# One-hot matrices stored by one edge pass and loaded by the next, and joined seams, in a four-layer graph stack on one core

## The reference

```python
h = jnp.maximum(_layernorm(x), 0.0);  x = x + L0(h, src, dst, ...)             # 3 attention layers, 4 heads
h = jnp.maximum(_layernorm(x), 0.0);  x = x + L1(h, src, dst, node_vec, ...)   # attention + scan, gated merge
h = jnp.maximum(_layernorm(x), 0.0);  x = x + L2(h, src, dst, edge_weight, ...)
h = jnp.maximum(_layernorm(x), 0.0);  x = x + L3(h, ...)
```

```python
s     = leaky_relu(a1[dst] + a2[src])
alpha = exp(s - max) / segment_sum(exp(s - max), dst)
agg   = segment_sum(alpha * ft[src], dst)
```

## Time and profile before

| | us |
|---|---|
| median of three runs | 8077.06 |
| the profiled execution, its own time | 8047.32 |
| its span | 8045.5 |
| busy: PE / DVE / POOL / ACT | 5416 / 5247 / 4576 / 3255 |
| L0's pass, gathers to last sum | 922 to 2640 |
| L1's pass with the scan | 3352 to 4960 |
| merge | 4961 to 5545 |
| L2's and L3's passes | 5558 to the end |

### The profile page before, as it was taken

One profiled execution on the slowest core, in us unless ns is written; L12 is line 12 of the kernel. 1 busy time (PEld: TensorE's weight loads), 2 busy tenths in 40 slices (PEclk: granted clock), 3 DMA queues, 4 the chain that ended last, 5 costly groups with the idle time before them and its releaser, 6 DMA issues. The chain is left out here.

```text
span 8045.5 us, 108971 instructions
## 1 busy us (share of the span) xinstructions
PE 5416.1 (67%) x20075; PEld 3414.8 (42%) x20075; DVE 5247.3 (65%) x11331; ACT 3255.3 (40%) x10996; POOL 4576.3 (57%) x4404
## 2 busy tenths in 40 slices
PE   4656788888888346477777774775566665566664
PEld 4523344444444232244444442564344443344443
DVE  7678588888888545698898984563455553333332
ACT  1224566666666225478787873441000000000000
POOL 4140266566665350287777774223777775777774
PEclk9988899999999658798998987897788887788887
DMA  7123577777777553477677776122444445344445
GB/s 256 23 71 107 184 241 243 239 241 243 245 243 219 183 176 96 157 235 243 239 249 241 248 227 147 62 69 72 118 142 142 140 142 96 112 136 136 136 135 88
DMA packets 481482, 1352.15 MB, mean 168 GB/s; under 512 B 129207, under 2 KB 220603, under 8 KB 480506
## 3 DMA queue, kind: packets, MB, share of 16 engines
q0 software_dynamic: 239680, 842.82, 36.1%
q1 hardware_dynamic: 198828, 436.55, 16.0%
q10 hardware_dynamic: 42668, 69.51, 2.8%
HBM read 1133.35 MB, written 546.45 MB: 209 GB/s over the span
## 5 line engine op out<-in xcount | busy, mean ns | idle before, releaser
L1190 POOL DMA_INDIRECT rows_e<-bundle,unit_src x1856 | 1775.2, 956 | 647.2 <-issue 542.2
L1211 PE MATMUL acc_e<-rows_e,hot_e 128*128 128x256 f32 x3712 | 1210.4, 475 | 920.7 <-DMA rows_e<-bundle,unit_src 746.1
L608 POOL DMA_INDIRECT rows_e<-table,unit_src x928 | 1027.6, 1107 | 840.8 <-PE acc_e L797 459.3
L797 PE MATMUL acc_e<-rows_e,hot_e 128*128 128x512 f32 (+1 forms) x3712 | 1343.0, 512 | 174.8 <-DVE rows_e L779 98.2
L967 POOL DMA_INDIRECT rows_e<-table,unit_src x928 | 1157.8, 1248 | 450.1 <-issue 247.1
L1211 PEld LDWEIGHTS acc_e<-rows_e,hot_e 128*128 128x128 f32 x3712 | 816.6, 234 | 1283.3 <-issue 618.7
L786 ACT ACTIVATE rows_e<-rows_e 128x64 f32<-128x64 f32 x4640 | 1119.0, 333 | 1.9
L797 PEld LDWEIGHTS acc_e<-rows_e,hot_e 128*128 128x128 f32 x3712 | 698.1, 195 | 746.3 <-issue 602.0
L1220 DVE SCALAR_TENSOR_TENSOR sums_e<-sums_e,unit_keep,acc_e 128x256 f32<-128x256 f32 x928 | 442.2, 477 | 736.0 <-PE acc_e L1211 730.8
L1053 ACT ACTIVATE rows_e<-rows_e 128x64 f32<-128x64 f32 x3712 | 919.9, 333 | 3.8
L2357 ACT ACTIVATE turned_f<-turn_f 128x512 f32<-128x512 f32 x98 | 58.5, 597 | 1893.2 <-PE turn_f L2355 1836.1
(11 more groups left out here) (444 smaller groups left out, 8525.6 us busy)
## 6 DMA issues: line engine op xcount, KB each, us to landing
bc<-bc_rows SPq DMA_DIRECT2D x226, 896.0 KB
summed<-sums_e SPq DMA_DIRECT2D x464, 390.0 KB
bundle<-sums_e SPq DMA_DIRECT2D x928, 128.0 KB
summed<-sums_e SPq DMA_DIRECT2D x464, 130.5 KB
given_f<-bundle ACTq DMA_DIRECT2D x98, 384.0 KB
rows_e<-table,unit_src POOLq DMA_INDIRECT x1856, 5.0
rows_e<-bundle,unit_src POOLq DMA_INDIRECT x1856, 2.7
summed<-zeros POOLq DMA_DIRECT2D x50, 390.0 KB, 17.6
```

The source lines that it names most:

```text
L608: pool.indirect_dma_start(self.rows[:, v, e, :], None, table, bass.IndirectOffsetOnAxis(unit_src[:, u, e:e + 1], 0)).then_inc(self.landed[ ...
L797: mm = pe.matmul(self.acc[:, v % 2, a0:a1], self.hot[:, v % self.SUMS, e, :], self.rows[:, v, e, a0:a1], start=(e == 0), stop=(e == 1))
L1190: pool.indirect_dma_start(self.rows[:, v, e, :], None, self.tab, bass.IndirectOffsetOnAxis(unit_src[:, u, e:e + 1], 0)).then_inc(self.land ...
L1211: mm = pe.matmul(self.acc[:, v % 2, 0:D], self.hot[:, v % self.SUMS, e, :], self.rows[:, v, e, :], start=(e == 0), stop=(e == 1))
```

## The change

- L0's `one_hot` makes the matrices in a ring of 8 units instead of 4, of which one half lies in the memory of `unit_w`. `unit_w` is therefore stored to DRAM before L0's pass (`w_kept`) and loaded again after it.
- SP stores every pair of units' matrices to DRAM (`hots`, 256 KB a store, 232 stores). DVE waits for the store before it writes over a pair.
- L1's pass has no `one_hot`; SP loads the matrices of four units at a time (512 KB, 116 loads) into a ring of 16 units, and PE waits for the load.
- In L1 `spread_top` stands ahead of `sum_rows` on PE, and `negate_top` at the end of DVE's slot.
- At the half's end, the copy of `y_ps` moves into the first step of the next half (after ACT's `decay`), the clearing matmuls behind that step's edge work on PE, and the gate loads behind the second step's `bc` load. Halves with c = 0 are written out too.
- Merge: the `settle` behind the weight loads goes; one gather of `y_all` is issued with each turn of the lanes; DVE, ACT and PE wait for the weights only where the first block needs `gat_b`. The DVE step on `unit_src` is done here.
- L2: only PE and DVE wait for the six weights. L2's and L3's passes use L0's semaphores for the landed rows again.

```diff
@@ SegmentPass (L0)
-                self.hot = lsb(f"hot_{name}", [P, self.SUMS, 2, P])
+                self.hot = (lsb(f"hot_{name}", [P, self.HOTS // 2, 2, P]),
+                            unit_w[:, :, :].rearrange("p (k u) e -> p k (u e)", k=self.HOTS // 2).rearrange(
+                                "p k (e n) -> p k e n", e=2))
...
+            def store_hots(self, i, v):
+                if v % 2 == 0:
+                    return
+                u, at_, half = i * RING + v, v % self.HOTS, self.HOTS // 2
+                sp.wait_ge(self.s_hot, u + 1)
+                sp.dma_start(hots[:, ds(u - 1, 2), :].rearrange("p u n -> p (u n)"), ...
+                             ).then_inc(self.hot_out[at_ // 2], 16)
...
             def one_hot(self, i, v):
                 u = i * RING + v
-                dve.wait_ge(self.s_pe, u + RING - self.SUMS + 1)
+                dve.wait_ge(self.s_pe, u + RING - self.HOTS + 1)
+                stored = RING // self.HOTS * i + v // self.HOTS
+                if v % 2 == 0 and (not isinstance(stored, int) or stored):
+                    dve.wait_ge(self.hot_out[v // 2 % (self.HOTS // 2)], 16 * stored)
...
                 self.behind(self.store_sums, self.STORE, i, v, edge)
+                self.behind(self.store_hots, self.WEIGH + 1, i, v, edge)
@@ ScoredPass (L1)
-            def one_hot(self, i, v): ...
+            def load_hots(self, i, v):
+                sp.dma_start(self.hot[:, v:v + self.LOAD, :, :].rearrange("p u e n -> p (u e n)"),
+                             hots[:, ds(i * RING + v, self.LOAD), :].rearrange("p u n -> p (u n)")
+                             ).then_inc(self.hot_in[v // self.LOAD % 2], 16)
...
-                pe.wait_ge(self.s_hot, u + 1)
+                k = v // self.LOAD
+                pe.wait_ge(self.hot_in[k % 2], 16 * (RING // self.LOAD // 2 * i + k // 2 + 1))
...
                 self.behind(self.store_sums, self.STORE, i, v, edge)
+                if v % self.LOAD == 0 and edge != "last":
+                    self.load_hots(i, v)
...
+                if j == 2 and edge != "last":
+                    self.spread_top(i, g)
                 self.behind(self.sum_rows, self.SUM, i, v, edge)
-                if edge != "last":
-                    if j == 1:
-                        self.turn_highest(i, g)
-                    elif j == 2:
-                        self.spread_top(i, g)
+                if j == 1 and edge != "last":
+                    self.turn_highest(i, g)
@@ scan
+            def copy_sum(half):
+                act.wait_ge(s_whole, half + 1)
+                act.wait_ge(s_gated, 2 * half + 2)
+                act.activation(y_sb..., y_ps[:, :, 0:HS], ACT.Copy).then_inc(s_copied, 1)
+
+            def clear_sum(half):
+                pe.wait_ge(s_copied, half + 1)
+                for z in range(2):
+                    pe.matmul(y_ps[:, z, 0:HS], zeros[:, 0:P], zeros[:, 0:HS], start=True, ...)
...
                     load_bc(STEPS * r + k + 2, k % 2)
+                    if w == 0 and k == 1:
+                        load_gate(half, g, c)
...
                     make_decay(r, k, m, 2 * f + c)
+                    if w == 0 and k == 0:
+                        copy_sum(half)
...
                     edges.pe_slot(i, v + 1)
+                    if w == 0 and k == 0:
+                        clear_sum(half)
                     add_up(r, k)
@@ merge
-        settle()
...
-            for t in range(T):
-                pool.indirect_dma_start(y_all[:, t, :], None, sorted_y, ...)
+            def return_rows():
+                for t in range(T):
+                    yield pool.indirect_dma_start(y_all[:, t, :], None, sorted_y, ...)
...
-            for e in (sp, pool, pe, dve, act):
-                chain.wait(e)
-                e.wait_ge(merge_loaded, 16 * (len(names) + len(sides) + 5))
+            chain.wait(act)
...
+                if b0 == 0:
+                    for e in (dve, act, pe):
+                        e.wait_ge(weights_here, all_loaded)
...
-            in_lanes(lanes, merge, 8)
+            in_lanes(lanes, merge, 8, return_rows(), 1)
@@ L2
-            chain.dma(sp, l1, l2, l3, l4, l5, l6)
+            for load in (l1, l2, l3, l4, l5, l6):
+                load().then_inc(weights_here, 16)
+            for e in (pe, dve):
+                e.wait_ge(weights_here, all_loaded + 16 * 6)
```

More of the change, by code:

```diff
@@ L215, in graph_stack_kernel @@
         key_row = scratch("key_row", [NP])
+        w_kept = scratch("w_kept", [P, UC * 2])
+        hots = scratch("hots", [P, UNITS, 2 * P])
         by_time = {n: scratch(f"scan_{n}", [P, 2, NP]) for n in ("xc", "dt", "dtx")}
@@ L907, in run @@
                 sp.wait_ge(self.masked[0], 16 * (n + 1))
+                for k in range(self.HOTS // 2):
+                    sp.wait_ge(self.hot_out[k], 16 * (UNITS // self.HOTS))
                 nc.all_engine_barrier()
@@ L940, in __init__ @@
                 self.landed = [sem(f"landed_{name}{v}") for v in range(G)]
+                self.hot_in = [sem(f"hot_in_{name}{k}") for k in range(2)]
                 self.stored = [sem(f"stored_{name}{v}") for v in range(self.SUMS)]
                 (self.s_score, self.s_row, self.s_run, self.s_top, self.s_neg, self.s_shrink, self.s_exp, self.s_keep,
-                 self.s_mark, self.s_hot, self.s_act, self.s_pe, self.s_sum) = (sem(f"{n}_{name}") for n in (
-                     "score", "row", "run", "top", "neg", "shrink", "exp", "keep", "mark", "hot", "act", "pe", "sum"))
+                 self.s_mark, self.s_act, self.s_pe, self.s_sum) = (sem(f"{n}_{name}") for n in (
+                     "score", "row", "run", "top", "neg", "shrink", "exp", "keep", "mark", "act", "pe", "sum"))
                 pe.sem_inc(self.s_pe, RING)
@@ L1114, in dve_slot @@
                 self.behind(self.collect, self.COLLECT, i, v, edge)
+                if j == 3 and edge != "last":
+                    self.negate_top(i, g)
             def act_slot(self, i, v, edge=None):
@@ L1172, in __init__ @@
                 self.acc = lps(f"acc_{name}", [P, 2, 512])
-                self.landed = [sem(f"landed_{name}{v}") for v in range(RING // 2)]
+                self.landed, self.seen = landed, seen
                 self.stored = [sem(f"stored_{name}{v}") for v in range(self.SUMS)]
@@ L2158, in scan_half @@
                 half = 2 * g + c
-                load_gate(half, g, c)
-                pe.wait_ge(s_copied, half + 1)
-                for z in range(2):
-                    pe.matmul(y_ps[:, z, 0:HS], zeros[:, 0:P], zeros[:, 0:HS], start=True, stop=False, skip_group_check=True)
-                if c == 0:
-                    with nc.Fori(0, MR // 2, engines=NOT_POOL) as w:
-                        scan_round(g, f, turn, c, w)
-                else:
-                    for w in range(MR // 2):
-                        scan_round(g, f, turn, c, w)
+                for w in range(MR // 2):
+                    scan_round(g, f, turn, c, w)
                 pe.wait_ge(s_x, 16 * (half + 1))
@@ L2188, in graph_stack_kernel @@
             load_dt(0, 0)
+            for z in range(2):
+                mm = pe.matmul(y_ps[:, z, 0:HS], zeros[:, 0:P], zeros[:, 0:HS], start=True, stop=True)
+            mm.then_inc(s_whole, 1)
             edges.begin()
```

71 lines of the change are left out of this document (36 added, 35 removed).

## The result

The changed kernel took 8032.95 us (median of five runs, 8021.56 to 8042.54) against 8077.06 (8074.52 to 8085.26): a ratio of 0.9942, 95% interval 0.9928 to 0.9957. In a later job it was 0.9915 (0.9899 to 0.9930). So 35 to 80 us were gained where 143 were forecast, and the time lies above the stated range.

What follows compares the result with a forecast made beforehand. The prediction took POOL's gathers and their stalls, next to DVE, to bound L1. Its terms -100 + 5 - 2 - 46 - 7 + 5 + 2 = -143 took the median 8077.06 to 7934 us, range 7900 to 7970 (wider: 7850 to 8015).

Steps and rivals of the forecast that it cites:

- The limits of L1: L1's main stretch: POOL, with some 28 us of stalls less, sets its length; 100 us gained of 1392.
- The forecast's -97: L1 from first to last scan: -100 for the main stretch, +5 and -2 at its end.
- +3: L1's end: +5 for hot loads into busy DMA engines, -2 for eight one-hots and the last waits.
- POOL's floor: L1's main stretch: POOL needs 1320 us at most, 6.35 a step, as `prod` and `inp` still stall gathers.
- rival D: L1: `bc` lands late, perhaps by 2 us in every step, making the kernel slower, 8113 us; chance 0.06.
- rival C: L0 and L1: DMA contention takes the gain; L1 gives 30, L0 costs 20, total 8019 us; chance 0.18.
- L0 and what lies around it: L0: +5 for gathers landing later beside the one-hot stores, +2 for `w_kept` and its return.
- Merge and L2: Merge: first power 54 us earlier, 7 to 8 given back, net -46; L2's first gather earlier, -7.
- Seams: L1's seams: `decay` ahead of the copy, waits fall under 2 us; nothing credited apart from the floors.

Runs made afterwards that it cites:

- experiment 7: Changed kernel with PE's sum ahead of `add_up` and the `bc` load split into two halves, each with nearly two steps to land; 7852.48 us, 0.9743 of before.
- experiment 6: Changed kernel with PE's sum in L1 one slot earlier, ahead of the step's `add_up`; 0.9871 of the kernel before.
- experiment 3: Changed kernel without its one-hot part: DVE makes one-hots in L1, no stores or loads, `unit_w` left alone; 0.9913 of the kernel before.
- experiment 8: As experiment 7, but DVE makes the one-hots in L1, with none stored or loaded; 0.9895 of the kernel before.
- experiments 5: The changed kernel itself, run again in a later job; 7997.62 us, 0.9915 of the kernel before.
- 10: As experiment 7, but with L1's halves separate and the spread of the maximum late, as before the change; 0.9804 of the kernel before.
- experiment 1: Changed kernel, but from L1's second round on each one-hot load brings 32 KB instead of 512 KB; 0.9940 of the kernel before.

## Why the prediction was wrong, step by step

- **The limits of L1 (the failed step).** I set a floor for each engine from its busy time and took POOL's, 1320 us less 28, for the length of the stretch. The runs showed two other limits in its place: a loop through the queues of PE and DVE (118.0 us of waits for the sum) and a transfer that is given one step to land (97.5 for `bc`). Neither is the busy time of an engine. A part of the loop had stood in the earlier trace rows, as 59.3 for the spread, and I let it go for nothing. I had written that `collect` "needs the same sum at about the same time", and then credited the gain all the same through the floors. Taking both limits away brings L1 down by 152 (experiment 7), taking the loop alone by 67 (experiment 6). The forecast's -97 became +3 in the first pair of profiles and 0 in the second: -16 and -5 in the thirteen halves, +19 and +5 in the last one, where I had +3.
- **POOL's floor.** It was no floor. I counted 1320 us with stalls that `prod` and `inp` cause and 28 that would go. The stalls per gather fell from 0.32 us to 1.099 - 0.945 = 0.15 with the one-hots, half of all. One-hots read two tensors from SBUF too, so the rule cited from the Trainium skill (SBUF — State Buffer, "SBUF: two separate sides") covers them; the trace agrees, and I had applied it only to the two longest. (By that section it holds only against an operation of GpSimd that reads SBUF; a gather reads its row numbers from `unit_src`.) Over the 208 steps before, a gather that ran beside none of the three took a mean 0.945 us (295 gathers), beside one-hots but neither `prod` nor `inp` 1.03 (172), beside `prod` or `inp` 1.63 (373); after the change the last kind took 1.23 (463). So most of what the one-hots cost showed where they stood next to `prod` and `inp`. How much a gather stalls also hangs on how dense DVE's work is: 1188 ns in experiment 3, 1325 in experiment 8, the same DVE work in a tighter order.
- **`bc` (rival D).** I had its window right, one step, and much of its cause, the hot loads; it got a chance of 0.06. Its price was too high: late by 2 us in every step was the estimate, and it was late in 68 waits with 97.5 us in the stretch. I had counted as a point against D that the hot load is issued before `prod` ends. All the same, 45 of the 68 waits are for loads issued behind a hot load.
- **Contention (rival C).** The DMA share rose to 0.81 in L1 and 0.85 in L0. The time given for C, 8019, is near the measured one, and a part of its mechanism is there, in the lateness of `bc`; the loop, the other part of what took the gain, is in no rival. A high share alone does no harm: in experiment 7 it is 0.92, with more time for each load to land.
- **L0 and what lies around it.** +7 forecast; +33 between the first pair of profiles to L1's first gather, +2 between the second, 17 to 20 by experiments 5, 7 and 8 of one job. Some 10 of it is, by the order in the code, `w_kept`: its store is issued at 923.05 and the first gather comes at 933.5, behind a barrier that I had not priced. The difference in L0's pass between kernels with and without the stores is -1 to +16.
- **Merge and L2.** 53 forecast, 46 and 51 found. The first power comes 26.0 us behind the weights' issue, by my working 21.4; `gat_b`'s add waits 7.12 for the last weight: it comes 21.9 behind the issue, where I had 11.5.
- **Seams.** The wait went, and the time with it only where nothing stood beside it: 34 us of L1, experiment 7 against 10.

## What to carry to other kernels

When an engine on the path is relieved, sort the loop's iterations by kind and follow one chain from a result back to its next use through every queue; a limit hidden beside the removed work may show only a part of itself as a wait. A transfer that hardly keeps anyone waiting may be landing just in time. Compare its landing time with the time from its issue to its use, and ask what both become when other transfers are added to its queue. Of two limits of one height each pays less alone than behind the other (67 and 85 here for early sums first and split loads behind them, about 20 for split loads alone), so an experiment on one alone can read as "no effect". And where a wait stays the same after an edit, see whether it is still the same wait: in experiment 1 late issues had taken the place of late landings.

## What the runs showed of the hardware

A gather's instruction on POOL took a mean of 1.08 to 1.33 us for the same bytes, by what DVE did meanwhile; beside nothing that reads two tensors from SBUF it takes 0.945. The scan reads two tensors as well, but its `decay` lies in PSUM, and the 242 gathers that ran beside it alone took a mean 0.95. In experiment 7 the DMA engines were busy to 0.92 at 303 GB/s, and in 1392 us DVE waited 24 us for the two halves of `bc` and PE 25 (three times) for a load of one-hots, so the share of 0.81 in the changed kernel was not its limit. A load of 896 KB landed a median 6.1 us after its issue where a load of 512 KB was issued ahead of it in the same queue, and 5.2 in the other steps. PE's clock was at its lower level for 259 of 1390 us in L1 of the changed kernel. Even steps took a mean 5.69 us with such time and 5.65 without, odd ones 7.89 and 7.22 (52 each); whether the clock makes the odd step long or the waits in it lower the clock no run here tells. In the first job single instructions of SP took 0.65 to 0.76 us, such as a move of 0.03 elsewhere, and held up the loads behind them.
